# Expert blocks 24 steps apart instead of 20 in the main stage, with their products, gates, turns and second products at steps of their own

## The reference, cut to what matters

```python
xn = layernorm(x)
scores = q @ k.T * 0.25 + slope * (j - i)       # 16 heads of 16, causal over 2048 tokens here
s = softmax(scores) @ v @ out_w.T + out_b
logits = xn @ gate_w.T + gate_b                 # 8 experts, the best two of each token, softmax over the two
h = xn @ w1[e].T + b1[e]                        # 512 columns, even ones glu, odd ones linear
y = glu * sigmoid(1.702 * glu) * (linear + 1) @ w2[e].T + b2[e]
x = x + s * silu(sum of the two weighted y)
```

## Time and profile before

| | |
|---|---|
| median of three runs | 816.44 us |
| the profiled execution's own time | 815.3 us |
| its span, first to last instruction | 813.5 us |
| busy: PE, DVE, ACT, POOL | 678.5 (83%), 601.9 (74%), 475.5 (58%), 279.3 us (34%) |
| chain that ended last | PE 55%, ACT 18%, DVE 13%, issue 7%, the rest 7% |
| store of a block to `y_rows`, issue to landing | 3.0 us |
| DVE `add_experts`, the two instructions | 346 and 652 ns (means) |
| DVE sum, reciprocal and division of a chunk | 441, 203 and 292 ns (means) |

### The profile page before, as it was taken

The page is one execution under the profiler, slowest core; times in us unless marked ns, Lnnn a source line. Parts: engine busy times, 40 slices in busy tenths (PEclk is TensorE's granted clock), DMA queues, the critical chain, the costliest instruction groups (busy, mean ns, idle before and its releaser), DMA issues.

```text
span 813.5 us, 14740 instructions
## 1 busy us (share of the span) xinstructions
PE 678.5 (83%) x5306; PEld 312.0 (38%) x5306; DVE 601.9 (74%) x1222; ACT 475.5 (58%) x990; POOL 279.3 (34%) x458
## 2 busy tenths in 40 slices
PE   3478859769889888989898898889898989898885
PEld 1234545433233433444344444443443443232432
DVE  5999776689777786787678777867886788688342
ACT  2276685860566575666565665666565656666551
POOL 2313442027723323333323433233333234660112
PEclk9889889985899999999999999999999999799998
DMA  9710324634450453244233323522442221350001
GB/s 293 251 65 0 97 73 160 200 130 149 161 145 1 124 152 87 71 124 125 72 86 127 93 74 111 148 83 79 134 127 72 80 90 46 88 185 14 27 32 47
DMA packets 76852, 85.84 MB, mean 106 GB/s; under 512 B 34169, under 2 KB 60284, under 8 KB 76412
## 3 DMA queue, kind: packets, MB, share of 16 engines
q1 hardware_dynamic: 71114, 74.05, 30.0%
q0 software_dynamic: 3280, 8.98, 3.5%
q10 hardware_dynamic: 2386, 1.87, 0.8%
HBM read 39.54 MB, written 27.53 MB: 82 GB/s over the span
## 4 chain that ended last, share of the span: by engine, by line
PE 55%; ACT 18%; DVE 13%; issue 7%; ACTq 3%; DMA 2%; SPq 1%; POOL 1%; POOLq 0%; DVEq 0%
PE bank L1575 16%; ACT PR L830 11%; PE bank L1511 9%; PE bank L1469 8%; DVE PM L1233 5%; PE bank L1534 5%; PE bank L1483 4%; PE bank L1341 3%; ACTq L811 3%; PE bank L1589 2%; PE bank L1384 2%; PE bank L1614 2%; ACT TG L788 1%; ACT U L819 1%; DMA qk_parts<-TG 1%
## 5 line engine op out<-in xcount | busy, mean ns | idle before, releaser
L830 ACT ACTIVATE PR<-bank 128x512 f32<-128x512 f32 (+3 forms) x640 | 317.1, 537 | 226.0 <-PE bank L1534 127.4
L1233 DVE TENSOR_REDUCE PM<-bank 128x1 f32<-128x512 f32 (+3 forms) x640 | 354.3, 604 | 73.6 <-PE bank L1511 46.4
L1534 PE MATMUL bank<-OPS 57*128 57x512 f16 (+3 forms) x640 | 209.6, 363 | 53.4 <-ACT PR L830 48.3
L1511 PE MATMUL bank<-OPS 54*128 54x512 f16 (+3 forms) x640 | 195.8, 372 | 10.5 <-DVE PM L1233 7.0
L1575 PE MATMUL bank<-PR,VS 128*17 128x512 f32 (+3 forms) x1280 | 161.2, 556 | 0.0
L1511 PEld LDWEIGHTS bank<-OPS 54*128 54x128 f16 x640 | 50.2, 95 | 129.6 <-DVE PM L1233 86.9
L1534 PEld LDWEIGHTS bank<-OPS 57*128 57x128 f16 x640 | 54.0, 94 | 117.6 <-ACT PR L830 109.1
L1469 PE MATMUL bank<-WB 128*128 128x256 f16 x552 | 81.2, 277 | 0.0
L600 POOL CAST POSB<-YT 128x256 f16<-128x256 f32 x46 | 18.2, 396 | 173.8 <-DVE YT L1135 173.8
L1469 PEld LDWEIGHTS bank<-WB 128*128 128x128 f16 x552 | 48.2, 98 | 32.5 <-issue 25.9
L1544 PE MATMUL bank<-MASK 64*128 64x64 bf16 x512 | 59.5, 199 | 0.0
(11 more groups left out here) (185 smaller groups left out, 893.2 us busy)
## 6 DMA issues: line engine op xcount, KB each, us to landing
WB<-W SPq DMA_DIRECT2D x23, 512.0 KB, 3.6
OPS<-qk_parts SPq DMA_DIRECT2D x60, 192.0 KB
x_rows<-PR SPq DMA_DIRECT2D x23, 256.0 KB, 3.3
WB<-in_w SPq DMA_DIRECT2D x23, 256.0 KB, 3.5
y_rows<-XT SPq DMA_DIRECT2D x23, 256.0 KB, 3.0
W<-in_w SPq DMA_DIRECT2D x6, 512.0 KB, 5.7
XT<-in_b SPq DMA_DIRECT2D x23, 128.0 KB, 3.9
XO<-in_x SPq DMA_DIRECT2D x4, 512.0 KB, 13.0
```

Of the source, the lines that this page charges most:

```text
L830: act.activation(PR[:, tile % RING, off:CH], PS[2 + tile % 2][:, off:CH], ACT.Exp, scale=1 / SCORE).then_inc(b_exped, 1)
L1233: dve.tensor_reduce(PM[:, c % 2, j, xq, gg:gg + 1], bank[:, 0:width], AX.X, ALU.max).then_inc(a_reduced, 1)
L1511: last = mm(bank[:, 0:width], OPS[ROWS_A, slot, 0, P * (TC * a + xq):P * (TC * a + xq) + P], OPS[ROWS_A, slot, 1, CH * gg:CH * gg + width] ...
L1534: last = mm(bank[:, off:CH], OPS[ROWS_B, slot, 1, P * k:P * k + P], OPS[ROWS_B, slot, 0, CH * b + off:CH * b + CH], start=True, stop=k < T ...
```

## The change

The blocks start earlier and are further apart (step 68 + 24 b, so the last one's second product moves from step 552 to step 628). Each part of the first product, six matmuls, is issued at one step, n, n + 4, n + 12 and n + 16; all these steps are multiples of 4, in which no value products stand. Tanh and gate, `glu` and `linear` get tables of their own: n + 6, n + 7, n + 9, n + 10 for half 0, and 12 more for half 1. The second product moves from n + 20 to n + 32, the fetch from n - 20 to n - 14. Turns of the sums move from 54 to 56 steps behind the chunk's end, onto multiples of 4; turns of maxima change for one of the first four chunks alone (two steps earlier). The gathers move from steps 564 to 624 (every fourth) to steps 634 to 679 (every third), behind the last store, and the additions of the experts move by 8 steps, from 630 to 675 to 638 to 683. `END_AT` stays.

```diff
-FIRST_BLOCK, EVERY = 92, 20
+FIRST_BLOCK, EVERY = 68, 24
...
-TURN_AT = {chunk_end(m) - 1 + (17, 17, 11, 5)[m] if m < NC else chunk_end(m) - 1 + 5: m for m in range(NC * PAIRS)}
-HEADS_AT = {chunk_end(m) - 1 + LEAD + 11: m for m in range(NC * PAIRS)}
+TURN_AT = {chunk_end(m) + ((16, 16, 8, 4)[m] if m < NC else 4): m for m in range(NC * PAIRS)}
+HEADS_AT = {chunk_end(m) + LEAD + 12: m for m in range(NC * PAIRS)}
 BLOCK_AT = {FIRST_BLOCK + EVERY * b: b for b in range(BLOCKS)}
-SPLIT_W_AT = {n + 4: b for n, b in BLOCK_AT.items()}
-SPLIT_Y_AT = {n + 8 + 9 * f: (b, f) for n, b in BLOCK_AT.items() for f in range(2)}
-DOWN_AT = {n + 20: b for n, b in BLOCK_AT.items()}
-FETCH_AT = {n - 20: b for n, b in BLOCK_AT.items()}
+UP_AT = {n + 12 * f + 4 * part: (b, f, part) for n, b in BLOCK_AT.items() for f in range(2) for part in range(2)}
+TANH_AT = {n + 12 * f + 6: (b, f) for n, b in BLOCK_AT.items() for f in range(2)}
+GATE_AT = {n + 12 * f + 7: (b, f) for n, b in BLOCK_AT.items() for f in range(2)}
+GLU_AT = {n + 12 * f + 9: (b, f) for n, b in BLOCK_AT.items() for f in range(2)}
+LINEAR_AT = {n + 12 * f + 10: (b, f) for n, b in BLOCK_AT.items() for f in range(2)}
+SPLIT_W_AT = {n + 3: b for n, b in BLOCK_AT.items()}
+SPLIT_Y_AT = {n + 12 * f + 11: (b, f) for n, b in BLOCK_AT.items() for f in range(2)}
+DOWN_AT = {n + 32: b for n, b in BLOCK_AT.items()}
+FETCH_AT = {n - 14: b for n, b in BLOCK_AT.items()}
...
-ADD_AT = {TOTAL - 10 + 3 * n: t
+ADD_AT = {TOTAL - 2 + 3 * n: t
...
-GATHER_AT = {PER_PAIR * (PAIRS - 1) + 4 + 4 * n: n for n in range(NT)}
+GATHER_AT = {TOTAL - 6 + 3 * n: n for n in range(NT)}
...
-                for f in range(2):
-                    for t in range(4):
-                        if n - t - 9 * f in BLOCK_AT:
-                            for j in range(3 * (t % 2), 3 * (t % 2) + 3):
-                                up(BLOCK_AT[n - t - 9 * f], f, t // 2, j)
+                if n in UP_AT:
+                    for j in range(6):
+                        up(*UP_AT[n], j)
```

More of the change, by code:

```diff
@@ L849, in _ @@
                         chunk_out(ended)
-                for f in range(2):
[L851 to L854, removed]
+                if n in TANH_AT:
+                    gate_tanh(*TANH_AT[n])
+                if n in GATE_AT:
+                    gate_linear(*GATE_AT[n])
                 if n - 1 in TURN_AT:
@@ L1293, in _ @@
                     sort(n + EXPERTS_KNOWN - 4)
[L1294 to L1298, removed]
+                if n in GLU_AT:
+                    glu(*GLU_AT[n])
+                if n in LINEAR_AT:
+                    linear(*LINEAR_AT[n])
                 if n - 1 in DOWN_AT:
```

## The result

| | before | after |
|---|---|---|
| median of the runs | 816.45 us | 857.02 us (851.35 to 864.36) |
| ratio, with its 95% interval | | 1.0462 (1.0406 to 1.0518) |
| span of the profiled execution | 813.5 us | 858.4 us |
| granted clock, mean over the span | 0.94 | 0.89 |

The kernel became 4.6% slower; the forecast was 800 us, in a range of 781 to 824. The ratio leaves out the slowest of the four runs after (864.36 us), which was over 1.5% above the fastest; the median has it. The spans differ by 44.9 us: 1.0 before step 68, 29.2 in steps 68 to 640 and 14.7 in the tail.

A forecast was written before the change was run, and what follows sets the result against it. No engine at its limit in steps 68 to 640 (PE nearest); the cost was put in bunched block work. 815.3 - 36 + 10.3 + 2 + 2 + 5 = 798.6, median 1.1 above: 800 us, range 781 to 824.

The forecast's parts named there:

- Later fetches: Main stage: fetches behind the next pair's loads (blocks 3 and 13) come late; +2 us, bounds 0 and 5.
- A block's price: Steps 68 to 640: a block costs 2.5 us instead of 4.07; 23 x 1.57 = -36 us, bounds 0 and -69.
- bunching: Steps 68 to 640: block work crowded into few steps starves DVE and ACT, then PE waits; carries a block's 4.07 us.
- First block and the clock after it: Step 68: PE waits for the first block's data, +10.3 us; then a few steps at half clock, +2 us.
- The tail: From S, the start of step 640: late gathers delay DVE's third `end_gate` and PE's fifth `end_turn`; +5 us, 0 to +16.5.
- The sum: Whole kernel: 815.3 - 36 + 10.3 + 2 + 2 + 5 = 798.6, median 1.1 above: 800 us.
- a block keeps its price: Main stage: a block stays near 4.07 us, as DVE and ACT have no room left; 836 us, chance 0.20.

The follow-up runs named there:

- rows16: The kernel after, with the source of the operand rows' loads rearranged so that its first dimension is 16 and not 3: 795.5 us, ratio 0.9726.
- no_loads: The kernel after, with the operand rows' loads left out from the third pair on: 801.8 us, ratio 0.9776.
- old_both: `rows16` with first products and gate on old offsets, and heads' turn and second product back on steps with value products: ratio 1.0068 to the kernel before.
- half_scatters: `rows16` with half of the scatters left out, so the first block's data is there earlier: 784.25 us, ratio 0.9559 to the kernel before.
- before_rows16: The kernel before, with only the loads' source rearranged to a first dimension of 16: 819.9 us, ratio 0.9990.

## Why the prediction was wrong, step by step

- **Later fetches, +2 us (0 to 5): the step that failed.** It measured 57 us in steps 120 to 600 (60 by the ratios): 40.4 of waits and 17.0 of longer busy time at the lower clock around them, which the term did not have at all. The place was right in part, for blocks 3 and 13 were named; blocks 10 and 20, one step behind the pair's second load, and 7 and 17 were not. The size failed because I took the fetch's 6.8 us as fixed, from one fetch that ran alone, and counted only the places in SP's list, not what a load in flight does to the fetch. Behind one the issue grew from 1.45 to as much as 8.3 us and the landing from 3.8 to 13.7. With the loads on all engines (`rows16`) or without them (`no_loads`) the six waits are gone, so the loads are shown to be the cause; whether they hold the fetch up in the engines alone is not.
- **A block's price, 4.07 to 2.5 us, -36 us.** 4.1 to 2.4 where nothing waits: 23 x 1.7, some -40 us. The mechanism, bunching, held, but its parts came out otherwise. The turns that leave the steps with value products were put at nothing; with the second products, which leave them too, they bring 0.6 us a block. The dearest of the earlier trace rows, a second product beside twelve first matmuls (2.35 us), is avoided in `old_both` too, which keeps only 0.4 of the gain.
- **First block and the clock after it, +10.3 and +2 us.** 13.7 us together by `half_scatters`; in the traces 11.6 (steps 68 to 80 of `rows16` take 20.9 us, before 9.3). Mechanism and size were right: the wait was 11.2 us in the kernel after and 9.3 in `rows16`.
- **The tail, +5 us (0 to +16.5).** +14.7 in the kernel after and +11.5 in `rows16`, within the bounds. I followed POOL's queue to DVE's third gate and PE's fifth `end_turn` (in the kernel after at S + 43.7 and S + 47.8, forecast S + 41.5 and S + 44), but missed DVE's first addition, which puts the gathers ahead of the last maxima, and the clock (0.78 in the tail, before 0.94).
- **The sum.** With the failed step taken out the kernel is `rows16`, forecast at 800 - 2 = 798 and measured at 795.5. That this is so close is partly luck: the blocks gained more than forecast and the tail lost more, each by some 4 to 7 us. The rival that ended on the slower side (a block keeps its price, 836 us) had the right side for a reason that did not occur.

## What to carry to other kernels

A transfer's duration read where it ran alone is not its price beside another one: look at the DMA share of what else is in flight, and at the worst landing, not the median. A regular schedule can hide a collision; before changing a period, list modulo the old one which transfers it kept apart. And a load whose DMA share is that of 3 of 16 engines is worth turning first where one line does it, even where it costs nothing yet (`before_rows16`).

## What the runs showed of the hardware that I had not expected

- Behind a load at a DMA share of 0.18, a transposing DMA took up to 8.3 us to issue instead of 1.3 where SP issued the load, and up to 8.5 where ACT did, and the issuing queue stood still meanwhile; ACT's own issue of two loads took 8.71 us in such a stretch.
- Six waits of PE for data, 40.4 us together, went with 17.0 us more of busy time for the same matmuls, at a granted clock of 0.93 against 1.00; at three of them the clock had fallen before the wait began.
